# Second attention gathered and normalised sequence by sequence, first experts in 39 slots with the low weights in halves

## The chip, the core and the metric

The kernel runs on one core of a Trainium2 chip. The metric is the device time of one execution in microseconds (us). The engines are TensorE (PE, with its weight loads as PEld), VectorE (DVE), ScalarE (ACT), GpSimd (POOL) and SyncE (SP). SP only issues transfers here; POOL computes and also issues the indirect transfers. Each engine runs its own instructions in order, and engines meet through semaphores that count up.

## What is computed

Input x has 8 sequences of 512 tokens, 256 wide. Four blocks follow, each on a layer-normed x and each added to x:

```
x = x + attention0(norm(x))          softmax attention, 16 heads of 16
x = x + experts0(norm(x))            8 experts, 1024 wide, each token goes to its best 2
x = x + attention1(norm(x))          cosine attention with running sums, and a 1024-wide MLP
x = x + experts1(norm(x))            64 small experts (best 8), 2 shared ones

experts0: out[token] = share0 * y[expert0] + share1 * y[expert1]
          y[e] = gelu(x @ w1[e] + b1[e]) @ w2[e] + b2[e]

attention1 on z = norm(norm(x) by ln1):
  q, k = tanh(z W_Q) * pi/4, tanh(z W_K) * pi/4 ; V = z W_V
  heads = (cos q * cumsum(cos k * V) + sin q * cumsum(sin k * V)) / (cos q * cumsum(cos k) + sin q * cumsum(sin k) + 1e-6)
  mixed = norm(x) + heads W_O
  result = mixed + gelu(norm(mixed) W1 + b1) W2 + b2
```

All products are done at float32 accuracy from reduced-precision parts: each matrix is split in a high part (a rounded copy) and a low part (what is left), and three products hi*hi, hi*lo, lo*hi are summed.

## The kernel before, in words

Every block is a phase with its own buffers, and a phase begins when all engines have ended the one before. The whole x stays on chip as 32 tiles of 128 tokens. Two of the five phases matter here.

**First experts** (`experts0_phase`). The router has sorted the tokens by expert into a list in DRAM, `sorted_x`. Each expert's part of the list is filled up to whole slots of 256 rows; there are SLOTS = 40 slots, and slot n belongs to expert `slot_expert[n]`, read at run time. A loop of TURNS = 20 turns does two slots a turn (k = 0, 1). For one slot:

- SP (`load`) fetches for the next slot: w1 of 1 MB when its buffer has been split (`w1_split`), then the slot's rows (256 KB), b1, b2 (128 KB), and w2 of 1 MB when its buffer has been split (`w2_hi`, `w2_lo`). There is one raw buffer for w1 and one for w2.
- DVE splits w1 (L1067 high, L1074 low, 128x2048 in one instruction), splits the hidden values in four pieces (L1056 high, L1058 low), and adds b2 (L1080).
- ACT does the gelu (L1100) and the high half of w2 (L1108), which waits for w2 to land.
- POOL does the low half of w2 (L1028), which waits for ACT's high half, and then stores the slot's results to `sorted_y` (L1030).
- PE does the first product (L1128), turns the next slot's rows (L991), and does the second product (L1141).

The last turn also fetches and splits for a 41st slot that nobody computes.

**Second attention** (`attention1_phase`). It starts by collecting the experts' results: POOL issues 64 indirect gathers (L1326), two for each of 32 tiles, into the buffers `zn` and `mixed` used as a ring of four. DVE adds them to x, weighted by `share` (L1389, two a tile), and takes statistics (L1392), for all 32 tiles in turn; between the tiles it takes the low parts of the five weight matrices (L1383). Then come, for all tiles at once, the aggregation (L1398), the first guess of 1/sqrt(variance) (L69, L71), three Newton steps on POOL (L79 to L85, twelve instructions), and after them the pipeline. PE waits for all five weights before its first product.

The pipeline has 64 chunks (8 sequences, 8 chunks of 128 value channels each) and 78 stages; stage n works on chunk n. With s = n // 8 and c = n % 8, a stage holds on DVE six instructions of one chunk (L1492, L1498, L1508), on PE `value(n + 1)`, `up`, `down` and `weigh`, on ACT and POOL the splitting of `heads` and `hidden`. Beside them each sequence has a front (its norm on DVE L1428, turned by PE L1638, q and k, the denominator) and a back (mixed L1456, its statistics L1461, its norm L1475, the MLP), and their steps are put at fixed values of c: front of s + 2 normed at c = 7; front of s + 1 at c = 1, 3, 5; back of s - 1 at c = 1, 2, 3; the sum of s - 2 at c = 4.

What DVE may not overtake: `weigh_queries(n, 0)` writes over `weighted`, which POOL must have added up for chunk n - 2 (`heads_ready`, L1357).

## Time and profile before

| | us |
|---|---|
| three runs | 3191.21, 3200.32, 3200.80 |
| median | 3200.32 |
| the profiled execution's own time | 3190.54 |
| its span | 3188.8 |
| mean granted TensorE clock | 0.908 |

| busy | us | share |
|---|---|---|
| PE | 2539.1 | 80% |
| DVE | 1845.6 | 58% |
| ACT | 1238.0 | 39% |
| POOL | 983.2 | 31% |

| stretch of the span | what | length, us | PE busy, us |
|---|---|---|---|
| 0 to 714 | first attention | 714 | 572.39 |
| 714 to 887 | router and sorting | 173 | 44.91 |
| 887 to 1438 | first experts | 551 | 483.75 |
| 1438 to 1571 | second attention up to its first stage | 133 | 15.35 |
| 1571 to 2176 | second attention, pipeline and end | 605 | 455.39 |
| 2176 to 3188 | second experts | 1012 | 967.34 |

How to read it: times are from the span's start. A share of busy time is an average over stages with different limits, so the last table is the one to begin with. In a timeline row the numbers are start, duration, then engine, line, operation, output and inputs, and in brackets the idle time of that engine just before and what ended it. Busy PE is not PE at its peak, since its ends are modelled.

### The profile page before, as it was taken

What the parts mean: (1) busy time and instruction counts of PE and PEld (TensorE: products, weight loads), DVE (VectorE), ACT (ScalarE), POOL (GpSimd) and SP (SyncE); (2) the same over time, 40 slices, a digit from 0 to 9 for tenths busy, and PEclk for the clock granted to TensorE, in tenths of its full rate; (3) what the DMA queues carried; (4) which work ended last, traced back from release to release, by engine and by line L of the source; (5) the groups of instructions that cost most, each with busy time, mean ns of one, the idle gap of its engine ahead of it and who ended that gap; (6) DMA issues with size and microseconds to landing.
All of it is one profiled execution on the core that took longest, in us unless ns stands there. A gap on an engine that the chain in (4) does not pass through costs nothing. (4 is left out here: it accounts for less than half of the span.)

```text
span 3188.8 us, 51896 instructions
## 1 busy us (share of the span) xinstructions
PE 2539.1 (80%) x18615; PEld 2207.7 (69%) x18615; DVE 1845.6 (58%) x3241; ACT 1238.0 (39%) x1845; POOL 983.2 (31%) x1102
## 2 busy tenths in 40 slices
PE   1988888885069999980368777785999999999999
PEld 1777667765068888880256666675788888888888
DVE  5455555545057777775597777744744544544543
ACT  0444444442034444441123333332444444444444
POOL 3444445401734444437244444451000000000000
PEclk9899999985589999995589999997999999999999
DMA  2000000003256666654354554423422222221321
GB/s 80 1 2 2 1 1 1 1 11 128 97 179 209 211 213 212 211 193 145 94 139 126 130 129 123 123 57 116 146 97 79 86 84 77 89 81 66 100 78 60
DMA packets 195231, 317.13 MB, mean 99 GB/s; under 512 B 28757, under 2 KB 103449, under 8 KB 195097
## 3 DMA queue, kind: packets, MB, share of 16 engines
q1 hardware_dynamic: 182856, 277.00, 28.9%
q0 software_dynamic: 12240, 38.28, 3.5%
q8 instruction: 92, 1.51, 0.2%
q14 instruction: 43, 0.34, 0.0%
HBM read 274.83 MB, written 40.37 MB: 99 GB/s over the span
## 5 line engine op out<-in xcount | busy, mean ns | idle before, releaser
L2015 DVE TENSOR_TENSOR e_h_lo<-e_h,e_h_hi 128x512 fp32r<-128x512 f32 x320 | 221.6, 692 | 481.2 <-ACT e_h_hi L2081 481.0
L2068 ACT ACTIVATE e_h<-e_h_ps,e_b 128x512 f32<-128x512 f32 x320 | 220.3, 688 | 491.7 <-PE e_h_ps L2132 461.1
L2146 PE MATMUL e_y_ps<-e_w_hi,e_h_hi 128*128 128x256 f32 x1280 | 366.3, 286 | 22.8 <-DVE e_h_lo L2015 22.7
L2146 PE MATMUL e_y_ps<-e_w_hi,e_h_lo 128*128 128x256 f32 x1280 | 361.7, 283 | 0.0
L2146 PE MATMUL e_y_ps<-e_w_lo,e_h_hi 128*128 128x256 f32 x1280 | 361.5, 282 | 0.0
L1028 POOL TENSOR_TENSOR e_w_lo<-e_w,e_w_hi 128x2048 fp32r<-128x2048 f32 x40 | 186.5, 4662 | 315.1 <-ACT e_w_hi L1108 315.1
L2146 PEld LDWEIGHTS e_y_ps<-e_w_hi,e_h_hi 128*128 128x128 f32 x1280 | 243.1, 190 | 54.5 <-DVE e_h_lo L2015 39.6
L2132 PE MATMUL e_h_ps<-e_yT_hi,e_w_hi 128*128 128x512 f32 x640 | 257.9, 403 | 2.5 <-DVE e_yT_lo L2001 2.5
L401 DVE TENSOR_REDUCE a_top<-a_ring 128x2 f32<-128x1024 f32 (+3 forms) x256 | 202.7, 819 | 90.2 <-PE a_ring L602 89.3
L2132 PE MATMUL e_h_ps<-e_yT_lo,e_w_hi 128*128 128x512 f32 x640 | 253.6, 396 | 0.0
L2132 PE MATMUL e_h_ps<-e_yT_hi,e_w_lo 128*128 128x512 f32 x640 | 253.1, 396 | 0.0
L2146 PEld LDWEIGHTS e_y_ps<-e_w_lo,e_h_hi 128*128 128x128 f32 x1280 | 243.1, 190 | 11.4
L2146 PEld LDWEIGHTS e_y_ps<-e_w_hi,e_h_lo 128*128 128x128 f32 x1280 | 244.4, 191 | 0.0
L79 POOL TENSOR_TENSOR e_newton<-e_rstd 128x4 f32<-128x4 f32 x24 | 6.1, 252 | 770.7 <-DVE e_rstd L71 769.4
L463 ACT ACTIVATE a_probs<-a_ring 128x1024 f32<-128x1024 f32 (+1 forms) x192 | 167.9, 883 | 139.9 <-PE a_ring L616 138.3
L2081 ACT ACTIVATE e_h_hi<-e_h 128x512 fp32r<-128x512 f32 x320 | 199.5, 623 | 46.1 <-DVE e_h L2012 44.3
L1128 PE MATMUL e_h_ps<-e_xT_hi,e_w_hi 128*128 128x256 f32 x640 | 183.7, 287 | 35.9 <-DVE e_w_lo L1074 30.9
L2012 DVE TENSOR_TENSOR e_h<-e_h,e_spread 128x512 f32<-128x512 f32 x256 | 175.3, 685 | 17.7 <-ACT e_h L2068 13.7
L1056 DVE CAST e_h_hi<-e_h 128x512 fp32r<-128x512 f32 x160 | 113.3, 708 | 118.3 <-ACT e_h L1100 113.3
L1141 PE MATMUL e_y_ps<-e_w_hi,e_h_hi 128*128 128x256 f32 x640 | 180.7, 282 | 0.5 <-DVE e_h_lo L1058 0.5
L1128 PE MATMUL e_h_ps<-e_xT_hi,e_w_lo 128*128 128x256 f32 x640 | 179.6, 281 | 0.0
L1128 PE MATMUL e_h_ps<-e_xT_lo,e_w_hi 128*128 128x256 f32 x640 | 179.5, 280 | 0.0
(364 smaller groups left out, 7078.1 us busy)
## 6 DMA issues: line engine op xcount, KB each, us to landing
e_w<-in_w SPq DMA_DIRECT2D x82, 1024.0 KB, 5.4
e_spread<-share_store SPq DMA_DIRECT2D x512, 128.0 KB, 2.9
a_keys<-rows_store SPq DMA_DIRECT2D x128, 256.0 KB, 5.1
a_queries<-rows_store SPq DMA_DIRECT2D x86, 256.0 KB, 4.5
a_running_hidden<-rows_store SPq DMA_DIRECT2D x42, 256.0 KB, 4.5
e_xs<-sorted_x SPq DMA_DIRECT2D x41, 256.0 KB, 4.9
sorted_x<-zeros POOLq DMA_DIRECT2D x10, 1024.0 KB, 16.9
sorted_y<-e_ys POOLq DMA_DIRECT2D x40, 256.0 KB, 4.8
```

Source lines behind the costliest of these rows:

```text
L401: dve.reduce_max(top[r % 2][:, tb, :], banks(k)[:, :, at:at + (tb + 1) * P], AX.X).then_inc(top_taken.sem, top_taken.tick())
L463: act.activation(probs[r % 3][:, :, B_AT[i]:B_AT[i] + B_WIDTH[i]], banks(k)[:, :, 0:B_WIDTH[i]], ACT.Exp).then_inc(probs_ready.sem, probs_ ...
L1028: pool.tensor_tensor(lo[:, :, :], w2[:, :, :], hi[:, :, :], ALU.subtract).then_inc(w2_lo.sem, w2_lo.tick())
L1056: dve.tensor_copy(h_parts[0][:, cut, :], h[:, cut, :]).then_inc(h_hi.sem, h_hi.tick())
L1128: last = pe.matmul(h_ps[:, at:at + SLOT_TOKENS], l, r, start=(m == 0), stop=(m == len(ops) - 1))
L1141: last = pe.matmul(y_ps[n][:, 0:D], h_parts[a][:, f, n * P:(n + 1) * P], w2_parts[k][w][:, f, :], start=(f == 0 and m == 0), stop=(f == FC ...
L2012: dve.tensor_tensor(h[:, c % 2, :], h[:, c % 2, :], spread[c % SPREADS][:, :], ALU.mult).then_inc(scaled.sem, scaled.tick())
L2015: dve.tensor_tensor(h_parts[c % 2][1][:, :], h[:, c % 2, :], h_parts[c % 2][0][:, :], ALU.subtract).then_inc(h_lo.sem, h_lo.tick())
L2068: act.activation(h[:, c % 2, :], h_ps[c % 2][:, :], ACT.Silu, bias=b1[:, c:c + 1]).then_inc(h_ready.sem, h_ready.tick())
L2081: act.activation(h_parts[c % 2][0][:, :], h[:, c % 2, :], ACT.Copy).then_inc(h_hi.sem, h_hi.tick())
L2132: last = pe.matmul(h_ps[c % 2][:, :], l, r, start=(m == 0), stop=(m == len(ops) - 1))
L2146: last = pe.matmul(y_ps[n][:, 0:D], h_parts[c % 2][a][:, n * P:(n + 1) * P], w2[b][:, c, :], start=False, stop=(c == CH - 1 and m == 2))
```

## The change

In the first experts:

- SLOTS is 39, the most that 8192 rows in 8 parts can need at 256 rows a slot. The loop runs 19 turns, and the 39th slot follows it, with no fetch and no split for a next one.
- The slot's rows are fetched first and have a semaphore of their own; they wait for PE to have turned the rows of the slot before. The transposes wait for the rows alone, no longer for b1 and b2.
- The low part of w1 is taken in two halves. PE begins a slot's first product after the first half, and waits for the second half before the fifth of eight hidden blocks.

In the second attention:

- Gathers, sums and statistics go by sequence of four tiles. Sequences 0 to 2 are done before the pipeline, sequence s + 3 during it: gathers on POOL at c = 4 and 5, sums on DVE at c = 5 and 6, spread at c = 7; its Newton steps at the next c = 0, its centre at c = 2.
- Both norms go from DVE to ACT, as scale and bias (bias from a small DVE instruction, `centre`, `centre2`): the front's at c = 7, the back's at c = 2 behind the angles.
- The five raw weights have buffers of their own and are all fetched at once. Their splits are spread: wqk, wv, wo before the pipeline, w1 and w2 at stages 1 to 4. PE waits for each where it first uses it.

Between first attention and router POOL clears a range of semaphores, so that their numbers can be used again.

```diff
-SLOTS = TOKENS * 2 // SLOT_TOKENS + E0
+SLOTS = (TOKENS * 2 + E0 * (SLOT_TOKENS - 1)) // SLOT_TOKENS
...
         def load(sp, slot, kn, free):
+            free("x")
+            sp.dma_start(xs[kn][:, :, :], rows_in[...]).then_inc(x_loaded.sem, 16)
             free("w1")
             sp.dma_start(w1[:, :, :], t["w1_0"][...]).then_inc(w1_loaded.sem, 16)
             free("rest")
-            sp.dma_start(xs[kn][:, :, :], rows_in[...]).then_inc(rest_loaded[kn].sem, 16)
...
-                        if what == "w1":
-                            sp.wait_ge(w1_split.sem, w1_split.at(2 * k, i))
+                        if what == "x":
+                            sp.wait_ge(x_transposed.sem, x_transposed.at(k, i))
+                        elif what == "w1":
+                            sp.wait_ge(w1_split.sem, w1_split.at(3 * k, i))
...
-                    dve.tensor_tensor(lo[:, :, :], w1[:, :, :], hi[:, :, :], ALU.subtract).then_inc(w1_split.sem,
-                            w1_split.tick())
+                    for f in halves:
+                        low_half(f)
...
+                for b in range(BANKS):
+                    if b in (0, BANKS // 2):
+                        pe.wait_ge(w1_split.sem, w1_split.at(3 * k - (b == 0), i))
...
+            with pe.Fori(0, TURNS) as i:
+                for k in range(2):
+                    slot(k, i, True)
+            slot(0, TURNS, False)
...
+            def gather(s, tiles):
+                for n in tiles:
+                    if s >= 4:
+                        pool.wait_ge(trB.sem, trB.at(KC, s - 4))
+                        pool.wait_ge(x_plus.sem, x_plus.at(TB, s - 4))
+                    elif s:
+                        pool.wait_ge(combined.sem, combined.at(4 * (n // 2 + 1), s - 1))
+                    for k in range(2):
+                        row = s * TB + n
+                        pool.indirect_dma_start(out=got(n, k), ...).then_inc(gathered[n].sem, 16)
...
+            gather(0, range(TB))
+            gather(1, range(2))
+            refine_front(0)
+            gather(1, range(2, TB))
+            gather(2, range(2))
+            refine_front(1)
+            gather(2, range(2, TB))
+            refine_front(2)
...
+                if c == 0 and s >= 1 and live(s + 2):
+                    refine_front(s + 2)
+                if c == 4 and live(s + 3):
+                    gather(s + 3, range(2))
+                if c == 5 and live(s + 3):
+                    gather(s + 3, range(2, TB))
...
+                if n in (2, 4):
+                    low_weights(3 if n == 2 else 4)
+                if c == 5 and live(s + 3):
+                    combine(s + 3, LEFT)
+                if c == 6 and live(s + 3):
+                    combine(s + 3, RIGHT)
+                if c == 7 and live(s + 3):
+                    spread_of(s + 3)
+                if c == 2 and s >= 1 and live(s + 2):
+                    centre_of(s + 2)
...
+            def norm_front(s):
+                act.wait_ge(centred.sem, centred.at(1, s))
+                if s:
+                    act.wait_ge(trF.sem, trF.at(KC, s - 1))
+                for n in range(TB):
+                    act.activation(zf[:, n, :], g.x[:, s * TB + n, :], ACT.Identity, bias=token(centre, s, n),
+                                   scale=token(twice, s, n)).then_inc(znF.sem, znF.tick())
...
+                if c == 2 and live(s - 1):
+                    norm_back(s - 1)
+                if c == 7 and live(s + 2):
+                    norm_front(s + 2)
```

**SyncE, loop of the first experts, one slot.** Before, the weights w1 go first, then the rows `e0_xs1`, the biases and w2:

```order
L976 DMA e0_w1<-in_w1_0 128x2x1024
L979 ISA
L979 DMA e0_xs1<-sorted_x 128x2x256
L981 ISA
L981 DMA e0_b1_1<-in_b1_0 128x8
```

Now the rows stand ahead of w1:

```order
L981 DMA e0_xs1<-sorted_x 128x2x256
L1011 ISA
L984 ISA
L984 DMA e0_w1<-in_w1_0 128x2x1024
L1017 ISA
L987 ISA
L987 DMA e0_b1_1<-in_b1_0 128x8
```

The rows moved from behind w1 to ahead of it, so in the queue they now follow the w2 of the slot before.

**VectorE, from the last gathered tile to the first stage of the second attention.** Before (the 31 tiles ahead of this one read the same), the spread of all 32 tiles follows the last tile, and then the front of sequence 0:

```order
L1389 SCALAR_TENSOR_TENSOR x<-a1_zn,share0,x 128x256
L1389 SCALAR_TENSOR_TENSOR x<-a1_mixed,share1,x 128x256
L1392 BN_STATS a1_stats<-x 128x6
L1396 COPY a1_half<-a1_stats 128x1
L1398 BN_AGGR a1_mv<-a1_stats 128x2 x32
...
L1428 TENSOR_SCALAR a1_values_heads<-x,a1_mv,a1_inverse 128x256 x4
L1434 TENSOR_TENSOR a1_frontT0_lo<-a1_yT,a1_frontT0_hi 128x512 x2
L1439 SCALAR_TENSOR_TENSOR a1_run<-a1_ones,a1_trig 48x512
L1442 TENSOR_TENSOR a1_run<-a1_trig,a1_run 48x512
L1447 RECIPROCAL a1_den<-a1_den 48x512
L1449 TENSOR_TENSOR a1_den<-a1_trig,a1_den 48x512
```

Now, from the centre of sequence 0 on (`a1_frontT0_lo` belongs to its front, the sums around it to sequences 1 and 2):

```order
L1483 SCALAR_TENSOR_TENSOR a1_centre<-a1_mv,a1_inverse 128x4
...
L1464 BN_STATS a1_stats<-x 128x6 x2
L1469 COPY a1_half<-a1_stats 128x1
...
L1495 TENSOR_TENSOR a1_frontT0_lo<-a1_yT,a1_frontT0_hi 128x512 x2
L1450 TENSOR_TENSOR a1_wv_lo<-a1_weighted,a1_wv_hi 128x2048
...
L1460 SCALAR_TENSOR_TENSOR x<-a1_zn,share0,x 128x256 x2
L1460 SCALAR_TENSOR_TENSOR x<-a1_mixed,share1,x 128x256 x2
L1464 BN_STATS a1_stats<-x 128x6 x2
L1500 SCALAR_TENSOR_TENSOR a1_run<-a1_ones,a1_trig 48x512
```

The front of sequence 0 starts after 4 tiles instead of 32, and the sums and statistics of sequences 1 and 2 stand between its steps.

**GpSimd, two stages of the pipeline (c = 4 and 5).** Before, a stage is the hidden split, the sum of the heads and their split:

```order
L1349 TENSOR_TENSOR a1_hidden_parts<-a1_running_hidden,a1_hidden_parts 128x512
L1357 TENSOR_TENSOR a1_values_heads<-a1_weighted 128x512
L1360 TENSOR_TENSOR a1_head_parts<-a1_values_heads,a1_head_parts 128x512
L1349 TENSOR_TENSOR a1_hidden_parts<-a1_running_hidden,a1_hidden_parts 128x512
L1357 TENSOR_TENSOR a1_values_heads<-a1_weighted 128x512
```

Now four gathers follow in each of the two:

```order
L1403 TENSOR_TENSOR a1_hidden_parts<-a1_running_hidden,a1_hidden_parts 128x512
L1411 TENSOR_TENSOR a1_values_heads<-a1_weighted 128x512
L1414 TENSOR_TENSOR a1_head_parts<-a1_values_heads,a1_head_parts 128x512
L1368 DMA a1_zn<-sorted_y,row0 128x256
L1368 DMA a1_mixed<-sorted_y,row1 128x256
L1368 DMA a1_zn<-sorted_y,row0 128x256
L1368 DMA a1_mixed<-sorted_y,row1 128x256
L1403 TENSOR_TENSOR a1_hidden_parts<-a1_running_hidden,a1_hidden_parts 128x512
L1411 TENSOR_TENSOR a1_values_heads<-a1_weighted 128x512
```

The sum of the heads, for which DVE waits two stages later, now stands behind four gathers.

## Rows read from the trace of the kernel before

**Rows 1.** Busy time by stretch: length, then PE, PEld, DVE, ACT, POOL.
```profile
887.00:1438.00 551.00, 483.75 (x4004) 467.94 (x4004) 406.00 (x523) 259.03 (x422) 218.99 (x83) 0.98 0.63 205
1438.00:1571.00 133.00, 15.35 (x38) 7.82 (x38) 69.84 (x169) 16.52 (x16) 70.45 (x76) 0.51 0.34 103
```

**Rows 2.** Waits in the first experts: total, times, longest, in us.
```profile
POOL e_w_lo L1028 <- ACT e_w_hi L1108: 315.1, 40, 9.0
PE e_h_ps L1128 <- DVE e_w_lo L1074: 30.9, 37, 1.0
```

**Rows 3.** Timelines of the engines, one slot of the first experts.
```profile
1183.81 0.38 SPq L984 DMA_DIRECT2D e_w<-in_w  x1
1189.75 2.28 DVE L1074 TENSOR_TENSOR e_w_lo<-e_w,e_w_hi 128x2048 fp32r<-128x2048 f32 x1
1190.16 1.92 ACT L1108 ACTIVATE e_w_hi<-e_w 128x2048 fp32r<-128x2048 f32 x1 [3.64 <-DMA e_w<-in_w]
1192.16 4.61 POOL L1028 TENSOR_TENSOR e_w_lo<-e_w,e_w_hi 128x2048 fp32r<-128x2048 f32 x1 [7.81 <-ACT e_w_hi L1108]
1192.26 0.38 PE L1128 MATMUL e_h_ps<-e_xT_hi,e_w_hi 128*128 128x256 f32 x1 [0.91 <-DVE e_w_lo L1074]
```

**Rows 4.** Issue to landing: w1 (L976), rows (L979), w2 (L984), gathers (L1326).
```profile
DMA to landing us min/median/max: 4.8/4.9/5.7
DMA to landing us min/median/max: 3.7/4.9/5.5
DMA to landing us min/median/max: 5.0/6.2/8.5
DMA to landing us min/median/max: 2.7/2.8/7.1
```

**Rows 5.** Timelines, end of the experts and start of the second attention.
```profile
1427.92 0.75 DVE L1080 TENSOR_TENSOR e_ys<-e_y_ps,e_b 128x256 f32<-128x256 f32 x2
1432.64 0.72 POOL L1030 DMA_DIRECT2D sorted_y<-e_ys  x1
1439.94 1.01 POOL L1326 DMA_INDIRECT a_zn<-sorted_y,row  x1 [6.57 <-POOLq L933]
```

**Rows 6.** Timelines of VectorE and GpSimd, gathers and first front.
```profile
1450.32 0.48 DVE L1389 SCALAR_TENSOR_TENSOR x<-a_zn,share,x 128x256 f32<-128x256 f32 x1 [4.66 <-DMA a_mixed<-sorted_y,row]
1466.05 2.28 DVE L1383 TENSOR_TENSOR a_wv_lo<-a_values_heads,a_wv_hi 128x2048 fp32r<-128x2048 f32 x1
1466.60 2.54 POOL L1326 DMA_INDIRECT a_mixed<-sorted_y,row  x1 [0.30 <-issue]
1524.68 0.94 POOL L1326 DMA_INDIRECT a_mixed<-sorted_y,row  x1 [0.30 <-issue]
1537.56 1.38 DVE L1428 TENSOR_SCALAR a_values_heads<-x,a_mv,a_inverse 128x256 f32<-128x256 f32 x4
1553.86 1.22 DVE L1439 TENSOR_TENSOR_SCAN a_run<-a_ones,a_trig 48x512 f32<-48x512 f32 x1 [9.45 <-ACT a_trig L1575]
1558.61 3.35 DVE L1447 RECIPROCAL a_den<-a_den 48x512 f32<-48x512 f32 x1 [2.81 <-ACT a_den L1579]
1571.14 0.70 DVE L1492 TENSOR_TENSOR a_run_ps<-a_v_ps,a_keys 128x512 f32<-128x512 f32 x1 [7.17 <-DMA a_keys<-rows_store]
```

**Rows 7.** Timelines of VectorE and GpSimd, one sequence in the pipeline.
```profile
1771.41 1.64 DVE L1456 SCALAR_TENSOR_TENSOR a_mixed<-x,a_inverse,a_wo_ps 128x256 f32<-128x256 f32 x4
1772.98 1.39 DVE L1461 BATCH_NORM_STATS2 a_stats<-a_mixed 128x6 f32<-128x256 f32 x4
1788.64 0.69 DVE L1508 TENSOR_TENSOR a_weighted<-a_run_ps,a_queries 128x512 f32<-128x512 f32 x1 [4.17 <-POOL a_values_heads L1357]
1806.57 1.27 POOL L1360 TENSOR_TENSOR a_head_parts<-a_values_heads,a_head_parts 128x512 fp32r<-128x512 f32 x1 [0.74 <-ACT a_head_parts L1612]
1825.62 0.69 DVE L1508 TENSOR_TENSOR a_weighted<-a_run_ps,a_queries 128x512 f32<-128x512 f32 x1 [2.34 <-POOL a_values_heads L1357]
1827.35 1.36 DVE L1428 TENSOR_SCALAR a_values_heads<-x,a_mv,a_inverse 128x256 f32<-128x256 f32 x4
```

More of the change, by code:

```diff
@@ L1021, in _, with store_slot @@
                                ALU.subtract).then_inc(w2_lo.sem, 1)
-            with pool.Fori(0, TURNS) as i:
-                for k in range(2):
+            def store_slot(k, i, slot, more):
+                if more:
                     pool.wait_ge(w2_hi.sem, w2_hi.at(k + 1, i))
@@ L1108, in _ @@
                     act.activation(w2_parts[1 - k][0][:, :, :], w2[:, :, :], ACT.Copy).then_inc(w2_hi.sem, w2_hi.tick())
+            with act.Fori(0, TURNS) as i:
+                for k in range(2):
+                    slot(k, i, True)
                 for sem in (h_ready, w2_hi, x_hi):
                     sem.close()
+            slot(0, TURNS, False)
         @block.tensor
         def _(pe):
-            pe.wait_ge(rest_loaded[0].sem, rest_loaded[0].at(0))
+            pe.wait_ge(x_loaded.sem, x_loaded.at(0))
@@ new lines, in combine @@
+            def combine(s, tiles):
+                first = 2 * tiles[0]
+                for k in range(2):
+                    for i, n in enumerate(tiles):
+                        if k == 0:
+                            dve.wait_ge(gathered[n].sem, 32 * (s + 1))
+                        else:
+                            dve.wait_ge(combined.sem, combined.at(first + i + 1, s))
+                        dve.scalar_tensor_tensor(out=g.x[:, s * TB + n, :], in0=got(n, k), scalar=token(g.share[k], s, n),
+                                                 in1=g.x[:, s * TB + n, :], op0=ALU.mult, op1=ALU.add).then_inc(combined.sem)
+                for i, n in enumerate(tiles):
+                    dve.wait_ge(combined.sem, combined.at(first + len(tiles) + i + 1, s))
+                    dve.bn_stats(stats[:, s % 2 * TB + n, :], g.x[:, s * TB + n, :]).then_inc(stat_step.sem)
@@ L1674, in up @@
             def up(u):
+                if u == 0:
+                    pe.wait_ge(split.sem, split.at(4))
                 if u % FC1 == 0:
```

374 lines of the change are left out of this document (209 added, 165 removed).

## The prediction, written before the changed kernel was timed

> **What bounds the kernel now.** I read the busy time by stretch first, since the two edited phases have different limits. The first experts last 551 us and TensorE is busy for 484 of them; the second attention spends 133 us before its first stage, with TensorE busy for 15 [rows 1]. So the first is close to TensorE's own pace, and in the second TensorE all but stands still, for which the timelines must give the cause.
>
> In the experts the waits come next. TensorE waits 37 times, 30.9 us in all, for the low part of w1; GpSimd waits 40 times for ScalarE's high part of w2 [rows 2]. The timelines of one slot tell which of the two sets the pace. w2 is asked for at 1183.81 and ScalarE can begin on it at 1190.16, 6.35 later; GpSimd's low part starts 2.00 after that and takes 4.61, and only when it ends may the next w2 be asked for [rows 3]. 6.35 + 2.00 + 4.61 and some 0.1 for the last step are 13.1 us, and 40 times that is 524 of the phase's 551 us. This ring of one raw w2 buffer goes round at its own pace; TensorE, which waits 0.91 in the slot shown [rows 3], is not in it.
>
> In the second attention I follow the chain back from the first stage at 1571.14. It waits 7.17 for the spread keys, and before that come the reciprocal at 1558.61, the running sum at 1553.86 (9.45 idle ahead of it) and the norm at 1537.56 [rows 6]. From norm to first stage are 33.6 us. Ahead of the norm stand the 64 gathers, from 1439.94 [rows 5] to 1524.68 [rows 6], 84.7 us, one every 1.25 when undisturbed (0.94 and 0.30 idle). GpSimd's gathers bound this stretch, and nothing of them is needed beyond the first four tiles to begin sequence 0.
>
> In the pipeline the timeline of VectorE shows where its work is covered: it waits 4.17 for the sum of the heads at 1788.64 (c = 3) and 2.34 at 1825.62 (c = 7) [rows 7].
>
> **The change, part by part.** The sum is made against the profiled execution's own 3190.54. The three runs lie at 3191 to 3201, so the profile is at their lower end, and a median of new runs may come up to 10 above my number.
>
> *One slot less.* The ring's 13.1 us go once: -13.1.
>
> *End of the experts.* Before, the last results were ready at 1428.67 (1427.92 + 0.75), but the store was issued at 1432.64, behind the low part of a w2 that nobody used [rows 5]. Now it follows at once: -4.0. The unrolled last slot is new code on every engine; no row shows its fetch. Bounds 0 and 4 (the longest fetch could be no longer than the 6.57 idle at the phase's start [rows 5], less what the barrier takes); I take +1.
>
> *w1 in halves.* TensorE can start a slot up to 1.0 earlier. What is late next is the ring above: GpSimd's low part of w2 cannot move, and VectorE and the second product follow it. So the gain is had once, not in every slot: -1.1. Both ends for the range: nothing, and 30.9 us if the ring shortens too (a rival). The w1 fetch waits for the second half, which ends when the whole did.
>
> *Rows ahead of w1.* They are now asked for behind the previous w2, in the same queue. Before, w1 and the rows issued right behind it both landed 4.9 after their issues, with w1 four times as large [rows 4]: the queue works them off in order, the rows last. Behind w2 they would then cost w2 nothing, and I take 0. The Trainium skill, "DMA: Bandwidth & Descriptors" (section "Queues, rings and completion order"), says that each transfer engine takes the descriptors of one ring in order; by this rule too the sum gets nothing here, and the rival below in which rows and w2 share would be out. I keep that rival, since no row shows this order of issue.
>
> Experts: -13.1 - 4.0 + 1 - 1.1 = -17.2.
>
> *Second attention up to the first stage.* The eighth gather is issued 7 x 1.25 after 1439.94, at 1448.7. Tile 1, whose last gather went out at 1443.7, was summed only at 1450.32 [rows 6], 6.6 later instead of the usual 2.8 [rows 4], because the weights were in flight; now five weights instead of three are asked for at once, so I add 3.8 for the eighth as well. From the last gather (1524.68) to the norm (1537.56) passed 12.9 us [rows 6]; with 28 fewer aggregations I estimate 10.9. The norm starts at 1448.7 + 3.8 + 10.9 = 1463.4. On ScalarE four tiles cost between 1.0 (half of the 1.92 for 128x2048, [rows 3]) and 2.0; I take 1.9 against VectorE's 1.38: +0.5. So the front moves by 1463.4 + 0.5 - 1537.56 = -73.7.
>
> Its cover: sums of sequences 1 and 2 now stand between its steps on VectorE. Sequence 1's second pair is gathered only behind GpSimd's Newton steps: four gathers from 1463.4, the last landing 3.75 + 2.8 later at 1470; two sums and statistics (about 2, [rows 7]) and a spread (1.2, estimate) bring 1473, where the low parts of the front would have begun near 1469.5. That is +3.5. Sequence 2's stand ahead of the reciprocal and cost about 0.5; the rest falls in the 9.45 and 7.17 of waiting. Gain before the first stage: -73.7 + 4.0 = about -70. Bounds: -60 (each of the two later groups late by one Newton and four gathers) and -76.
>
> *In the pipeline,* five sequences get eight sums (2 x 1.64), four statistics (1.4), a spread (1.2) and small centres (0.5): 6.4 us of VectorE each [rows 7]. The front's norm of 1.36 goes from c = 7 [rows 7]. The back's goes too, but it and the centres lie ahead of the 4.17 wait, so they count nothing. The 2.34 wait at c = 7 disappears under the new work. 6.4 - 0.5 - 1.4 - 2.3 = 2.2; I add 0.5 for the wait on the last gather's landing and 0.8 since ScalarE must do the back's norm behind the angles, late for the next hidden chunk: +3.5, four times. In sequence 0 no hidden chunks run, there is nothing to absorb, and two low weights of 2.28 each [rows 6] come in: 6.0 - 1.4 + 4.6 = +9. On GpSimd the four gathers (5.0) start when the heads' split ends at 1807.84 (1806.57 + 1.27, [rows 7]) and end at 1812.8, when the next hidden split is due about then. Total +23; bounds +5 (all else absorbed) and +73 (both groups of gathers exposed, below).
>
> Second attention: -70 + 23 = -47. Clearing semaphores and one transfer less of zeros are not on a path that the router waits for: 0.
>
> Sum: 3190.5 - 17.2 - 47 = 3126.
>
> **Rivals.**
>
> *The ring shortens too.* If w2 lands sooner because the rows no longer run ahead of it (its landings span 5.0 to 8.5, [rows 4]), the slot falls from 13.1 toward TensorE's own 12.1. Against it: w2 takes 6.2 at the median, also where w1 went out earlier. At 12.3 and 38 slots: -30, 3096. Chance 0.13.
>
> *Rows and w2 share.* The rows, a quarter of w2's size, delay it by up to a quarter of 4.9; at half of that, 0.6 in 38 slots: +23, 3149. Against it the in-order landing above. Chance 0.09.
>
> *GpSimd binds at c = 4 and 5.* If the sum of the heads behind the gathers is late, VectorE waits 5 us twice in each of five sequences: +50, 3176. For it: the 2.34 and 4.17 waits show that these sums are late already. Against it: VectorE itself gets 4.8 us more there. Chance 0.11.
>
> *The other side: gathers held up by VectorE.* A gather took 2.54 instead of 0.95 when it was issued inside a VectorE instruction of 2.28 [rows 6]. In the pipeline VectorE is nearly always in an instruction. If each of 8 gathers takes 2.84 with its gap, that is 22.7 us a sequence on GpSimd, of which I let 4 be covered: +93, 3219, slower than before. It decides from about 1.9 us of exposed time per gather. Against it: the instructions there are under 1.3 us long but for the reciprocal. The Trainium skill, "SBUF — State Buffer" (section "Who interferes with whom"), says that copies, casts and tensor-scalar forms can lock GpSimd out, and that a tensor-tensor does not stop descriptor writing. By that rule the gathers at c = 4 and 5 would run free and this rival would be out; the row disagrees, since what ran there was a tensor-tensor [rows 6], and the measurement decides. Chance 0.05.
>
> **How the numbers follow.** Forecast 0.62, the rivals 0.13, 0.09, 0.11 and 0.05. The time is the forecast's, 3126. Its own range is 3112 to 3142. The whole range, 3085 to 3168, takes in the first two rivals and leaves out the last two, 0.16. A measurement of this kernel can tell about 0.3%, 9.6 us, from no change. All cases but the last are faster: 0.94; same 0.02; slower 0.04.
>
> **What would show it.** Right: 39 low parts of w2 some 13.1 apart; TensorE's wait on w1's low part gone and found again ahead of the second product; the store right behind the last sums; first stage about 62 us after the first gather; sequences 1 to 4 of the pipeline 3 to 4 us longer than before, sequence 0 about 9. Wrong: slots clearly under 12.8 or over 13.4; gathers in the pipeline above 1.5 us; VectorE waits on the heads of over 4 us at c = 6 or 7; or a first stage later than 75 us after the first gather.

## The result, and the profile after

| | kernel before | changed kernel |
|---|---|---|
| runs, median | 3191.2 us (9 runs, 3182.6 to 3200.8) | 3168.1 us (9 runs, 3159.4 to 3183.3) |
| ratio, 95% interval | | 0.9928 (0.9905 to 0.9952) |
| profiled execution, its span | 3190.5, 3188.8 us | 3170.1, 3168.3 us |

The change is worth about 23 us by the medians, 15 to 30 by the interval; the forecast was 3126 us, a gain of 64, and its range ended at 3168. So the prediction was wrong in size: two thirds of the gain did not come.

To find where it went I cut each trace at the same three instructions: SP's first fetch of the first experts, GpSimd's first gather, and VectorE's first instruction of the last phase.

| us | before | after | difference | forecast |
|---|---|---|---|---|
| up to the first experts (not edited) | 887.4 | 884.2 | -3.2 | 0 |
| first experts, to the first gather | 552.6 | 540.4 | -12.2 | -17.2 |
| first gather to first stage | 131.2 | 61.2 | -70.0 | -70 |
| first stage to the last phase | 605.0 | 669.5 | +64.5 | +23 |
| last phase (not edited) | 1012.7 | 1013.0 | +0.3 | 0 |

The first row is no part of the change: over the fourteen profiles of this study this unedited stretch took 876 to 897 us. That is much of why whole times of one kernel spread by 20 us and more, and why I compare the stretches. The edited ones give 17.7 of the 20.5 us between the two profiles.

A stretch repeats better, but not exactly. The unedited attention took 736.2 before and 741.1 in e3_experts_only below; of kernels that share one attention, the changed kernel, e4 and e8 took 730.7, 731.2 and 728.4. So a difference of a few us between two profiles needs a second sign, such as a wait that went or a chunk that shrank.

The busy time by stretch of the changed kernel (length, then PE, PEld, DVE, ACT, POOL, granted clock, DMA share, GB/s), for the experts and the stretch up to the first stage, answers to [rows 1]. TensorE is busy for 480 of the 540 us of the experts, as it was for 484 of 551, and still for only 14 us ahead of the first stage, but of 61 instead of 133:

```profile
884.10:1424.50 540.40, 479.75 (x3900) 462.03 (x3900) 442.17 (x551) 246.50 (x409) 206.90 (x80) 0.97 0.60 200
1424.50:1485.80 61.30, 13.96 (x38) 7.02 (x38) 32.97 (x91) 16.52 (x22) 34.00 (x60) 0.56 0.44 137
```

The waits in the experts (total, times, longest) answer to [rows 2]. TensorE's wait for w1's low part is gone from the list, and one of the same size stands ahead of the second product instead. In e8_no_halves below it is the other way round (32.8 for the first product, 2.9 for the second), so the halves only moved it.

```profile
POOL e_w_lo L1034 <- ACT e_w_hi L1130: 302.9, 38, 10.6
PE e_y_ps L1170 <- DVE e_h_lo L1070: 34.8, 72, 0.9
```

The timelines of the start of the second attention (start, length, engine, line, operation, idle time before and what ended it) answer to [rows 5, 6]. The store goes out at 1417.45, behind the last sum; the first norm, now ScalarE's, begins 23.4 us after the first gather (forecast 23.5) and takes 2.07; the first stage follows 61.2 us after the gather (forecast 62).

```profile
1417.45 0.71 POOL L1036 DMA_DIRECT2D sorted_y<-e_ys  x1 [7.30 <-DVE e_ys L1096]
1424.59 1.01 POOL L1368 DMA_INDIRECT a_zn<-sorted_y,row  x1 [6.43 <-POOLq L935]
1447.95 2.07 ACT L1648 ACTIVATE a_values_heads<-x,a_centre,a_inverse 128x256 f32<-128x256 f32 x4 [18.02 <-DVE a_centre L1483]
1473.58 3.35 DVE L1507 RECIPROCAL a_den<-a_den 48x512 f32<-48x512 f32 x1
1485.83 0.70 DVE L1551 TENSOR_TENSOR a_run_ps<-a_v_ps,a_keys 128x512 f32<-128x512 f32 x1 [5.84 <-DMA a_keys<-rows_store]
```

The loss is in the pipeline. I took the start of VectorE's first instruction of each chunk (L1492 before, L1551 after) and wrote down the distance to the next one. Sequence 3, in us; each kernel's name stands for its experiment below:

```
                   c=0   c=1   c=2   c=3   c=4   c=5   c=6   c=7   sequence
before             4.6  15.3   5.9  16.0   9.4   8.8   4.6   9.4     74.0
after              4.6  15.5   4.8  19.1   9.6  17.8   6.9   7.0     85.3
e1_sums_later      4.6  17.9   4.8  17.7   9.5   8.9   6.9  11.5     81.8
e2_back_norm       4.6  15.5   6.1  16.8  10.0  18.3   6.9   7.0     85.2
e5_stats_in_wait   4.6  17.3   4.8  19.0   9.8   8.8   6.2  10.4     81.0
e6_stats_and_norm  4.6  15.7   6.1  16.7  10.1   8.8   6.2  10.2     78.5
e7_no_sums         4.6  17.0   4.8  17.6   9.5   8.9   5.7  12.2     80.4
e9_gathers_earl.   4.6  15.5   4.8  19.0   9.5  11.3   6.9   6.8     78.5
e10_all_earlier    4.6  15.7   6.1  16.8   9.8   8.9   6.2   7.5     75.6
```

Sequences 2 and 4 of the changed kernel differ from this by at most 0.9 in a chunk. Chunk 5 alone is 9.0 longer than before, 8.9 in sequence 2. The timeline of VectorE and GpSimd there, in sequence 2, shows it at work:

```profile
1675.65 0.97 POOL L1368 DMA_INDIRECT a_zn<-sorted_y,row  x1
1676.93 0.95 POOL L1368 DMA_INDIRECT a_mixed<-sorted_y,row  x1 [0.30 <-issue]
1678.09 1.22 DVE L1557 TENSOR_TENSOR_SCAN a_v_ps<-a_ones,a_v_ps 128x512 f32<-128x512 f32 x1
1684.01 1.25 DVE L1460 SCALAR_TENSOR_TENSOR x<-a_zn,share,x 128x256 f32<-128x256 f32 x1 [4.70 <-DMA a_mixed<-sorted_y,row]
1686.47 0.48 DVE L1460 SCALAR_TENSOR_TENSOR x<-a_zn,share,x 128x256 f32<-128x256 f32 x1 [1.21 <-DMA a_mixed<-sorted_y,row]
1686.87 0.88 DVE L1460 SCALAR_TENSOR_TENSOR x<-a_mixed,share,x 128x256 f32<-128x256 f32 x2
1687.66 0.74 DVE L1464 BATCH_NORM_STATS2 a_stats<-x 128x6 f32<-128x256 f32 x2
1688.32 3.32 DVE L1507 RECIPROCAL a_den<-a_den 48x512 f32<-48x512 f32 x1
1692.29 0.68 DVE L1551 TENSOR_TENSOR a_run_ps<-a_v_ps,a_keys 128x512 f32<-128x512 f32 x1
```

The gather itself takes 0.95, as in the stretch ahead of the pipeline. But the rows of tile 0, asked for at 1676.93, are there only at 1684.0, and the first sum stands in VectorE's row ahead of the reciprocal and of chunk 6. Two waits, 4.70 and 1.21, and the sums and statistics of two tiles, 1.64 + 0.74, are 8.3 of the 8.9. TensorE stands still with it; from its timeline, and the busy time by stretch from 1675 on:

```profile
1693.62 0.80 PE L1737 MATMUL a_v_ps<-a_frontT_hi,a_wv_hi 128*128 128x512 f32 x1 [11.29 <-DVE a_weighted L1567]
```
```profile
1675.00:1684.00 9.00, 6.41 (x38) 5.58 (x38) 4.31 (x6) 1.95 (x3) 7.12 (x8) 1.00 0.74 161
1684.00:1691.50 7.50, 0.00 (x0) 0.00 (x0) 6.29 (x7) 0.00 (x0) 4.79 (x5) 0.59 0.31 89
1691.50:1700.00 8.50, 6.38 (x21) 5.23 (x22) 8.46 (x16) 0.82 (x2) 0.00 (x0) 0.56 0.38 114
```

TensorE does nothing in the 7.5 us, and the granted clock, at its upper level (2.4 GHz, 1.00) before, is 0.59 and 0.56 in this stretch and the next, near its lower level (1.2 GHz): the first product takes 0.80, where the one at 1675.92 took 0.51.

Why the rows come late has two parts. One is in the transfers issued from 1675.0 to 1680.5, and from 1685.0 to 1690.0 (KB each, median us from issue to landing):

```profile
a_running_hidden<-rows_store SPq DMA_DIRECT2D x2, 256.0 KB, 5.8
a_keys<-rows_store SPq DMA_DIRECT2D x2, 256.0 KB, 7.0
a_zn<-sorted_y,row POOLq DMA_INDIRECT x2, 5.6
a_mixed<-sorted_y,row POOLq DMA_INDIRECT x2, 7.0
```
```profile
a_zn<-sorted_y,row POOLq DMA_INDIRECT x2, 2.8
a_mixed<-sorted_y,row POOLq DMA_INDIRECT x2, 2.8
```

Beside four spreads of queries and keys, 1 MB together, a gather lands in 5.6 to 7.0 us. The second group, with no spread beside it, lands in 2.8, the number of [rows 4] that I had worked with. SP sends spreads out once a chunk, behind VectorE; the second group went out while VectorE stood still. At 1761 to 1765, in sequence 3, the first group reads 6.0 and 6.8. That the spreads slow the rows is read from such coincidences; no run takes the spreads away.

The other part is that the gathers are issued too late for the sums, whatever the landing. Sequence 1 shows it by itself. Its first group went out 6.0 us after the start of chunk 5 (1.1 in sequences 2 to 4), with no spread issued beside it, and VectorE waited 4.30 all the same (the gathers of 1592 to 1598, then the rows of GpSimd and VectorE):

```profile
a_zn<-sorted_y,row POOLq DMA_INDIRECT x2, 3.2
a_mixed<-sorted_y,row POOLq DMA_INDIRECT x2, 2.8
```
```profile
1594.25 0.95 POOL L1368 DMA_INDIRECT a_mixed<-sorted_y,row  x1 [0.30 <-issue]
1597.04 3.86 DVE L1460 SCALAR_TENSOR_TENSOR x<-a_zn,share,x 128x256 f32<-128x256 f32 x2 [4.30 <-DMA a_mixed<-sorted_y,row]
1597.73 1.27 POOL L1403 TENSOR_TENSOR a_hidden_parts<-a_running_hidden,a_hidden_parts 128x512 fp32r<-128x512 f32 x1
```

In sequence 2 VectorE stood ready at 1679.31, and the second gathers of the two tiles went out at 1676.93 and 1679.44. With 2.8 to each landing it would have waited 0.4 and then 2.1, so 2.5 of the 5.9 (an estimate from these rows). Done for all five sequences this gives 14.7 of the 28.0 us that VectorE waits for rows in the pipeline: about half is the slow landing and about half the late issue.

### The profile page after: what moved, and what is told of

The parts are those of the page before. It is cut to its first block and busy times, and to the rows that moved or that the text cites. A ratio compares the mean times of both kernels' runs of the same rounds, so it can differ in the third digit from the quotient of the medians.

```text
span 3168.3 us, 51829 instructions
## 1 busy us (share of the span) xinstructions
PE 2551.7 (81%) x18511; PEld 2213.6 (70%) x18511; DVE 1859.1 (59%) x3264; ACT 1256.2 (40%) x1896; POOL 987.4 (31%) x1182
## 5 line engine op out<-in xcount | busy, mean ns | idle before, releaser
L1034 POOL TENSOR_TENSOR e_w_lo<-e_w,e_w_hi 128x2048 fp32r<-128x2048 f32 x38 | 175.6, 4622 | 302.9 <-ACT e_w_hi L1130 302.9
L2270 PEld LDWEIGHTS e_y_ps<-e_w_lo,e_h_hi 128*128 128x128 f32 x1280 | 243.4, 190 | 11.3
L1068 DVE CAST e_h_hi<-e_h 128x512 fp32r<-128x512 f32 x156 | 153.3, 983 | 71.7 <-ACT e_h L1122 67.1
L2136 DVE TENSOR_TENSOR e_h<-e_h,e_spread 128x512 f32<-128x512 f32 x256 | 175.3, 685 | 17.8 <-ACT e_h L2192 13.6
L1737 PE MATMUL a_v_ps<-a_frontT_hi,a_wv_hi 128*128 128x512 f32 x128 | 62.6, 489 | 141.1 <-DVE a_weighted L1567 141.0
```

The lines of the kernel that those rows point to most:

```text
L1034: pool.tensor_tensor(lo[:, :, :], w2[:, :, :], hi[:, :, :], ALU.subtract).then_inc(w2_lo.sem, w2_lo.tick())
L1068: dve.tensor_copy(h_parts[0][:, cut, :], h[:, cut, :]).then_inc(h_hi.sem, h_hi.tick())
L2136: dve.tensor_tensor(h[:, c % 2, :], h[:, c % 2, :], spread[c % SPREADS][:, :], ALU.mult).then_inc(scaled.sem, scaled.tick())
L2270: last = pe.matmul(y_ps[n][:, 0:D], h_parts[c % 2][a][:, n * P:(n + 1) * P], w2[b][:, c, :], start=False, stop=(c == CH - 1 and m == 2))
```

## The experiments

The kernel before ran beside them: 20 runs at 3186.3 us (median) beside the first four kernels, 9 at 3190.8 beside the next four, 7 at 3189.5 beside the last four. Ratios are to these, each with its 95% interval. In the paragraphs below "attention" is the stretch from the first gather to the last phase (736.2 before, 730.7 after), "experts" the one ahead of it (552.6 and 540.4).

**e1_sums_later.**

```
-                if c == 5 and live(s + 3):      combine(s + 3, LEFT)
-                if c == 6 and live(s + 3):      combine(s + 3, RIGHT)
-                if c == 7 and live(s + 3):      spread_of(s + 3)
+                if c == 6 and live(s + 3):      combine(s + 3, LEFT)
+                if c == 7 and live(s + 3):      combine(s + 3, RIGHT); spread_of(s + 3)
```

> The changed kernel with the sums of a sequence's rows on VectorE one chunk later: first two tiles after chunk 6, last two and the spread after chunk 7; gathers stay after chunks 4 and 5 on GpSimd. Theory A (VectorE stands at the gathers' landing, 4.2 + 1.2 us in each of five sequences, with everything behind it): the interval that begins at chunk 5 falls from 17.7 to about 11, five sequences gain 5 to 7 us each, and the kernel comes to about 3168 - 30 = 3138 us. Theory B (GpSimd binds: its four gathers, 5.0 us, hold up the sum of the heads and the split of the hidden chunk): the wait only moves from the gathers' landing to the heads' sum, VectorE waits 4 to 6 us for the heads in chunk 5 or 6, and the kernel stays at 3160 to 3170 us.

Measured 3149.6 us, 0.9878 (0.9842 to 0.9915); attention 717.3, 13.4 less than after. The landing wait fell from 28.0 to 5.3 us in the pipeline, and chunk 5 returned to 8.9. So the wait was real and did not simply move to the heads, against B. But A's 30 did not come either: chunk 7 grew by 4.5 and the next chunk 1 by 2.4. Moving the sums only moved them to where they are not hidden.

**e2_back_norm_vector.** The four ScalarE norms of the back (`norm_back`) are four tensor-scalar operations on VectorE again, as in the kernel before.

> The changed kernel with the second norm of each sequence back on VectorE (four tensor-scalar operations instead of ScalarE's four, and no centre). Theory A (ScalarE's norm stands ahead of the hidden chunk and the high parts in its row, and costs 1.5 to 3 us in each sequence at chunks 2 and 3): about 8 to 12 us faster than the changed kernel, 3157 us, and VectorE's wait for the high part of the back channels falls from 23.8 to about 9 us. Theory B (the longer stage at chunk 3 comes from elsewhere, ScalarE's time is covered): within 3 us of the changed kernel.

Measured 3166.2 us, 0.9931 (0.9899 to 0.9963), no different from the changed kernel as a time. By the trace the attention is 6.3 shorter (724.4): chunk 3 shorter by 2.3 to 3.2, chunk 2 longer by 1.2 (2.5 in sequence 1), and the wait for the high part of the back channels 11.6 instead of 23.8. The mechanism is A's by the chunks and the wait; its size, a little under the 8 to 12 expected, is known to a few us only, and the wait for rows grew meanwhile from 28.0 to 32.9.

**e3_experts_only.** `attention1_phase` of the kernel before, all else as changed.

> The kernel before with the edits of the first experts alone (39 slots, rows asked for first, low weights in halves); the second attention is the old one. If the two parts of the change add up, this is 12 us faster than the kernel before (the ring at 13.2 us goes round once less, -13.2; store earlier -3.7; a slower start and a slightly slower ring +5), 3179 us, and the attention's part is the remaining -11. My forecast had -17 for this part. A rival: the clock or the memory of the attention depends on what ran ahead, and this part alone is worth over 17 or under 8.

Measured 3178.6 us, 0.9974 (0.9956 to 0.9992). The experts took 543.0, 9.6 less than before. The time is 7.7 us less than that of the kernel before beside it, where 12 were expected and under 8 was the rival's; the unedited attention took 4.9 more than in the profile before, and I can't tell this from the spread of that stretch. So the parts add up roughly, and the experts are not worth 17.

**e4_rows_behind_w1.** In `load`, the rows' transfer stands behind w1's again.

> The changed kernel with the rows asked for behind w1 as before; halves and 39 slots stay. Theory A (rows asked for between w2 and w1 take part of the transfer time of w2 and of the first w1): the ring goes round in 13.12 instead of 13.19 us and the first slots start 1.5 to 2 us earlier, 3 to 5 us in all, and w2's wait on ScalarE falls back from 4.9 to about 3.6 us per slot. Theory B (transfers of one queue come strictly one after the other): the ring's period stays at 13.19, and nothing changes by over 1 us, or it gets slower since the transposes wait for the rows again.

Measured 3173.6 us, 0.9967 (0.9946 to 0.9988). In the trace the experts took 540.4, exactly as in the changed kernel: ring 13.16 instead of 13.18, ScalarE's wait for w2 142 instead of 181 us, the second step 21.1 instead of 19.5. So the order of rows and w1 is worth nothing. The wait fell as A has it, but not for A's reason: w2 landed 6.2 us after its issue at the median, 6.3 in the changed kernel, and ScalarE waits just 145 us in e8, where the rows are ahead too. The long wait comes only with halves and rows ahead together, and the ring does not follow it. Against its own comparison this kernel gains 12.7 us where the changed kernel gained 23.1. The 10 us between them are not in any stretch that was edited; the unedited first one took 2.9 us more in this profile than in that of the changed kernel, and where the rest came from I leave open.

**e5_stats_in_wait.** As e1, but `combine` of sequences 3 to 7 only sums, and

```
                 if c == 1 and live(s + 1):
                     front(s + 1, m, "low0")
+                    if s >= 1 and live(s + 2):
+                        stats_of(s + 2, range(TB)); spread_of(s + 2)
                     front(s + 1, m, "low1")
  (GpSimd)
-                if c == 0 and s >= 1 and live(s + 2):   refine_front(s + 2)
+                if c == 1 and s >= 1 and live(s + 2):   refine_front(s + 2)
```

> The kernel of the first experiment (sums after chunks 6 and 7), and in addition the statistics and the spread of the sequence that is three ahead stand after chunk 1 of the next sequence, between the two low parts of the front channels, where VectorE waits 3.5 us for ScalarE; GpSimd's Newton steps for them follow at chunk 1 instead of chunk 0. Theory A (with the landing wait gone, VectorE is the bound of chunks 5, 6, 7 and 0, every instruction there costs its length, while chunks 1 and 3 have waits to hide it in): chunk 7's interval falls from 11.5 to about 8.5 and chunk 1's from 17.9 to 15.5, 5 us in each of four to five sequences, 3128 us. Theory B (GpSimd's row binds: hidden split, heads, Newton steps in order): the heads of chunk 1 come later by the 3.4 us of the steps, and the kernel stays within 5 us of 3149.

Measured 3142.1 us, 0.9834 (0.9786 to 0.9882); attention 706.0, 11.3 less than e1. The wait for the front's high part fell from 19.6 to 4.8 us: the statistics are hidden there. Half of what A expected came; chunk 7 stayed at 10.4.

**e6_stats_and_norm.** e5 with e2's norm.

> The kernel of the fifth experiment with the second norm back on VectorE, as in the second experiment. There it shortened the pipeline by about 1.2 us in each sequence (chunk 3 shorter by 2.4, chunk 2 longer by 1.2). If that adds up, this is 6 to 9 us faster than the fifth experiment, 3120 us; a rival: VectorE has no wait left at chunk 2 and 3 once the statistics moved, and it is no faster.

Measured 3136.3 us, 0.9829 (0.978 to 0.9877); attention 701.2. It adds up in part, 4.8 by the stretch, which is no more than the unedited attention moved in e3; the chunks go the way they went in e2: in sequences 2 to 4 chunk 3 is shorter by 0.8 to 2.3 and chunk 2 longer by 1.2.

**e7_no_sums.** In e1's `combine`, for s >= 3: a copy of one element in place of the sum.

> The kernel of the first experiment without the eight sums (scalar-tensor-tensor, 128x256) of each of sequences 3 to 7: a copy of one element stands for each, so gathers, waits, statistics and all else stay, and the results of these sequences are those of the rows without the experts' share. It prices the sums. Theory A (VectorE binds there): 8 x 0.41 less 8 x 0.06 = 2.8 us a sequence, five times, 14 us, about 3135 us. Theory B (GpSimd's gathers bind): within 3 us of the first experiment, 3147 to 3150.

Measured 3148.0 us, 0.9854 (0.9806 to 0.9901); attention 710.5, 6.8 less than e1. 14 us of VectorE's work were taken away and half of it came back. Chunk 7 of sequence 3 did not shrink, 12.2 (in sequences 2 and 4 it lost 0.9), VectorE's wait for the heads grew from 48.0 to 52.6 us, and its wait for the rows, which the small copies keep, from 5.3 to 10.2. So VectorE met GpSimd's results and the landing earlier, and waited for both: neither theory alone.

**e8_no_halves.** The changed kernel with `halves = [slice(0, F0)]` and the semaphore's counts to match.

> The changed kernel with the low part of w1 in one instruction of 128x2048 again; 39 slots and rows first stay. Theory A (the ring of w2 sets the pace, halves are worth one step at most, and the slow start of the experts comes from how VectorE's and GpSimd's low parts meet): ring still 13.1 to 13.2 us, TensorE waits 0.8 us a slot for w1's low part again, and the time is within 3 us of the changed kernel. Theory B (the halves do shorten something in every slot): 5 to 10 us slower.

Measured 3160.8 us, 0.9912 (0.987 to 0.9953). Experts 536.3: 4.1 *less* than with the halves, where I expected none. The timelines of VectorE and GpSimd in the second slot, first the changed kernel, then e8:

```profile
910.81 4.55 POOL L1034 TENSOR_TENSOR e_w_lo<-e_w,e_w_hi 128x2048 fp32r<-128x2048 f32 x1 [7.94 <-ACT e_w_hi L1130]
911.10 6.47 DVE L1074 TENSOR_TENSOR e_w_lo<-e_w,e_w_hi 128x1024 fp32r<-128x1024 f32 x2
917.50 0.74 DVE L1096 TENSOR_TENSOR e_ys<-e_y_ps,e_b 128x256 f32<-128x256 f32 x2
917.75 0.37 SPq L984 DMA_DIRECT2D e_w<-in_w  x1
```
```profile
907.96 2.29 DVE L1074 TENSOR_TENSOR e_w_lo<-e_w,e_w_hi 128x2048 fp32r<-128x2048 f32 x1
907.99 6.73 POOL L1034 TENSOR_TENSOR e_w_lo<-e_w,e_w_hi 128x2048 fp32r<-128x2048 f32 x1 [8.26 <-ACT e_w_hi L1130]
910.42 0.37 SPq L984 DMA_DIRECT2D e_w<-in_w  x1
```

The two halves should take 2.35 and took 6.47: one of them lasted 5.34 and ended with GpSimd's low part. In e8 VectorE was 0.03 ahead and GpSimd waited. w1's fetch, which waits for the split, goes out 6.65 after VectorE's start in the one and 2.46 in the other. In the nine other kernels with halves the pair took 6.36 to 6.78 too, also where VectorE's first half came first: then GpSimd got in between the halves and the second waited. The next low part of w2 came after 19.2 to 19.6 us (21.1 in e4) with halves, and after 15.2 to 15.5 without (16.3 in the kernel before). In later slots the two are not due together, and it costs nothing.

**e9_gathers_earlier.** One difference to the changed kernel:

```
-                if c == 4 and live(s + 3):   gather(s + 3, range(2))
-                if c == 5 and live(s + 3):   gather(s + 3, range(2, TB))
+                if c == 3 and live(s + 3):   gather(s + 3, range(2))
+                if c == 4 and live(s + 3):   gather(s + 3, range(2, TB))
```

> The changed kernel with one difference: GpSimd issues the gathers of the pipeline after chunks 3 and 4 instead of 4 and 5; VectorE's sums stay after chunks 5 and 6. Theory A (the loss at chunk 5 is the landing of rows gathered too late): VectorE's wait of 5.4 us a sequence for the gathers goes, chunk 5's interval falls from 17.7 to 11.5, and the kernel gains some 25 to 30 us of the pipeline, less what sums at chunk 5 cost, 3140 us. Theory B (GpSimd binds): its row is as long as before, the heads of chunk 4 come late instead, chunk 4 grows by 3 to 5 us, and the gain is under 12 us.

Measured 3135.2 us, 0.9838 (0.9812 to 0.9865); attention 702.8, 27.9 less than the changed kernel. It is A's number, and the largest effect of one edit here. VectorE's waits in the pipeline from 1485 to 2000 us (total, times, longest), of the changed kernel and of e9:

```profile
DVE a_weighted L1567 <- POOL a_values_heads L1411: 41.7, 16, 6.0
DVE x L1460 <- DMA a_mixed<-sorted_y,row: 28.0, 9, 4.7
```
```profile
DVE a_weighted L1567 <- POOL a_values_heads L1411: 45.4, 18, 5.9
DVE x L1460 <- DMA a_mixed<-sorted_y,row: 2.9, 2, 1.8
```

The heads wait 3.7 us more over the whole pipeline, and chunk 4 did not grow. The wait for rows fell by 25.1. This profile has no landing times, but by the two waits that are left, in sequences 0 and 1, rows still took 6.3 and 7.0 us (asked for at 1514.3 and 1579.1). So the landing can be as slow as it was; the earlier issue hides it. In e9's chunk 5 the same instructions run without a gap:

```profile
1663.29 1.22 DVE L1557 TENSOR_TENSOR_SCAN a_v_ps<-a_ones,a_v_ps 128x512 f32<-128x512 f32 x1
1664.41 0.85 DVE L1460 SCALAR_TENSOR_TENSOR x<-a_zn,share,x 128x256 f32<-128x256 f32 x2
1665.19 0.87 DVE L1460 SCALAR_TENSOR_TENSOR x<-a_mixed,share,x 128x256 f32<-128x256 f32 x2
1665.98 0.74 DVE L1464 BATCH_NORM_STATS2 a_stats<-x 128x6 f32<-128x256 f32 x2
1666.64 3.33 DVE L1507 RECIPROCAL a_den<-a_den 48x512 f32<-48x512 f32 x1
```

**e10_all_earlier.** e6 with e9's gathers.

> The kernel of the sixth experiment (sums after chunks 6 and 7, statistics at chunk 1, back norm on VectorE) with GpSimd's gathers after chunks 3 and 4 instead of 4 and 5. Without the sums at all chunk 7 still took 10.6 to 12.2 us, so something of GpSimd is in it: its five us of gathers after chunk 5 push the heads of chunks 6 and 7. Theory A (that is so): chunk 7 falls from 10.2 to about 8, chunk 6 stays at 6.2, and 2 us are gained in each of five sequences, about 10 us, 3126 us. Theory B (chunk 7 is bound by VectorE and TensorE alone): no gain, 3133 to 3138 us.

Measured 3128.0 us, 0.9815 (0.9785 to 0.9846); attention 688.4, 12.8 less than e6. Chunk 7 fell from 10.2 to 7.5, A's number, but the timeline does not show A's mechanism. VectorE and GpSimd in chunk 7 of sequence 3, first e6, then e10:

```profile
1759.49 0.69 DVE L1572 TENSOR_TENSOR a_weighted<-a_run_ps,a_queries 128x512 f32<-128x512 f32 x1 [0.70 <-POOL a_values_heads L1411]
1763.58 0.69 DVE L1460 SCALAR_TENSOR_TENSOR x<-a_zn,share,x 128x256 f32<-128x256 f32 x1 [1.89 <-DMA a_mixed<-sorted_y,row]
1763.93 1.46 POOL L1411 TENSOR_TENSOR a_values_heads<-a_weighted 128x512 f32<-128x512 f32 x1
1764.19 1.88 DVE L1460 SCALAR_TENSOR_TENSOR x<-a_mixed,share,x 128x256 f32<-128x256 f32 x2
```
```profile
1754.76 0.69 DVE L1572 TENSOR_TENSOR a_weighted<-a_run_ps,a_queries 128x512 f32<-128x512 f32 x1 [0.90 <-POOL a_values_heads L1411]
1757.27 0.87 DVE L1460 SCALAR_TENSOR_TENSOR x<-a_mixed,share,x 128x256 f32<-128x256 f32 x2
```

The heads are waited for as long as before, 0.70 and 0.90. What went is the wait for rows, 1.89, and the stretching of the sums: the last two take 1.88 beside a GpSimd tensor-tensor in e6 and 0.87 in e10. On average over sequences 2 to 4, chunk 7 loses 1.6 of waiting for rows and 1.5 of longer sums. Later sums fall together with GpSimd's work, and earlier rows take them out of its way. That they meet is read from the timelines; no run parts the two.

**e11_no_halves.** e6 with e8's edit.

> The kernel of the sixth experiment with w1's low part in one instruction. The halves cost 4 us once, in the second slot of the experts (GpSimd's low part of w2 got in between them, and VectorE's second half took 5.3 us instead of 1.2): without them the third low part of w2 follows the second after 15.5 instead of 19.5 us, and the kernel is 4 us faster than the sixth experiment, 3131 us. A rival: the 4 us come back as a wait later in the ring, and the time is the same.

Measured 3130.7 us, 0.9815 (0.9797 to 0.9834). Experts 535.0, 5.1 less than in e6, so the gain of e8 is there again and does not come back as a wait; the attention is 702.6, as in e6.

**e12_both.** e10 with e8's edit.

> The tenth and eleventh experiments together: sums after chunks 6 and 7, statistics at chunk 1, back norm on VectorE, gathers after chunks 3 and 4, w1's low part in one instruction. If both add to the sixth experiment: 3121 us, some 70 us less than the kernel before. A rival: gathers after chunk 3 wait for the transposes of the back norm and hold up the heads of chunk 4, and it is no better than the eleventh.

Measured 3117.7 us, 0.9773 (0.9752 to 0.9794), 72 us less than the kernel before: the best version found. Experts 534.6, attention 689.5, so both parts are there. The rival is out: this kernel is 13 us faster than e11, and chunk 4 takes 9.5 to 9.7 in sequences 2 to 4, where it takes 9.9 to 10.1 in e11. The ratio to the changed kernel is 0.9773 / 0.9928 = 0.984, by way of the kernel before, since the two did not run side by side.

## Why the prediction was wrong

*One slot less, store, new code: right in sum.* -13.1 by the ring, which went round in 13.18 us against 13.12. The store followed the last sum (1416.39 + 0.76) after 0.3, where it had been 4.0 late. Two small misses cancel, which was luck: 0.06 more a turn is 2.2 us over the slots, and from the last low part of w2 that was used to the first gather passed 5.2 us less than before, where I had 4.0 less and 1 more for new code. No cost of new code shows there.

*w1 in halves: wrong sign.* I took -1.1, once. It cost 4.1, once, in the second slot. Nothing in [rows 3] shows it, since there VectorE's low part had ended when GpSimd's began; I priced a split as harmless without asking who uses the pause. The trace of the kernel before had the warning in its second slot: GpSimd's low part, begun 0.11 us behind VectorE's, took 6.66 instead of 4.62. The experts without halves came to -16.3 (e8), against -16.1 in my sum, so this is the whole of what they missed.

*Rows ahead of w1: right, 0.* e4's stretch is the same to 0.1, and w2 landed as soon with the rows ahead of it.

*Up to the first stage: right.* -70 forecast, -70.0 measured, and with the steps in between: norm 23.4 after the first gather.

*In the pipeline: this step failed.* +23 forecast, +64.5 measured. It failed in two sentences. The first was "I add 0.5 for the wait on the last gather's landing". VectorE waits 4.3 to 6.7 us a sequence for rows, 28.0 in all, and e9, which changes nothing but the issue of the gathers, takes 27.9 away. I had looked only at when GpSimd would have issued the gathers and at the last one. The first pairs decide, because the first sums stand in VectorE's row ahead of the reciprocal and of the next chunk. Even at the 2.8 of [rows 4] they would have come some 2.5 us late in a sequence; and they travel with 1 MB of spreads and take up to 7.1, which is the other half. I had even used a row with this behaviour, the landing of 6.6 "because the weights were in flight", for the start and not for the pipeline.

The second was that ScalarE's norm of the back costs 0.8, in four sequences. With it on ScalarE a sequence is longer by about 1.2 at chunks 2 and 3, in the later sequences too (e2: 6.3 in all).

What is left, 64.5 - 27.9 - 6.3 = 30.3, stands against the rest of my sum: 23 less four times 0.5 + 0.8 is 17.8. These 12.5 us are not settled. Some of them are in sequences 5 to 7 and the end, which take in no rows and for which I had put nothing: they are 7.1 longer than before, and e2 takes about 3 of these away. Some may be VectorE's sums, which I priced at 0.41 each: the first of sequence 1, in the rows above, lasted 3.47 beside GpSimd's tensor-tensors (the pair of sums is the 3.86 of the row). Some may be no more than the spread of the stretch.

By sequence the sum was not bad once the gathers are in time. In e9 sequences 0 to 4 are 11.2, 5.9, 5.1, 4.5 and 4.2 longer than before, where I had 9 and four times 3.5; in the changed kernel it is 12.9 (8.4 of it at chunk 5), 11.3, 11.7, 11.3 and 10.2.

*The rivals.* "GpSimd binds at c = 4 and 5" gave 3176, near the time, and I had 0.11 on it. That it came near is luck, since its mechanism is not the one that decided: VectorE's wait for the heads in the pipeline grew by 6.6 us, from 47.5 to 54.1, not by 50, and the wait for rows is new. In one way GpSimd is in it, since it issued the gathers late (sequence 1). "Gathers held up by VectorE" is out: they took 0.94 to 1.20. "Ring shortens" and "rows and w2 share" are out: the ring is as it was, and so is the landing of w2. I had no rival in which VectorE waits for the rows. Under "what would show it" I named waits on the heads and long gathers, but not a wait of VectorE on the transfer.

The forecast for the attention, -47, was reached by e10 (-47.8). That it agrees to the microsecond is chance, since e10 also hides the statistics (e5), which my sum had not. But the gain was to be had; it was the placement that gave it back.

## What to carry to other kernels

When a transfer is moved from a quiet stretch into a pipeline, look at which instruction waits for its first bytes, when that instruction is ready, and what is queued behind it, and price the landing with what else is in flight there. A move of the issue by one step cost nothing and was worth 28 us; moving the consumer instead was worth half (13.4), since it landed in a part where its engine had no slack and GpSimd was at work. Find the slack first (chunks of 15 to 19 us had it, those of 4.6 had none) and put there what may go anywhere. Cutting an instruction in two opens a door between the parts, and another engine may come in by it.

## What the runs showed of the hardware

A low part on VectorE and one on GpSimd (tensor-tensor, both inputs on chip) do not run at the same time. The one that begins second lasts until the first has ended, and then its own time: 6.73 instead of 4.62 on GpSimd in e8, 5.34 instead of 1.22 on VectorE after the change, with 0.03 to 0.4 us between the starts. The Trainium skill, "SBUF — State Buffer" (section "Who interferes with whom"), says that a VectorE instruction with two such inputs contends with a GpSimd instruction that reads, and that the order of issue decides who blocks; these rows agree. The sums (scalar-tensor-tensor, 128x256) are stretched by GpSimd's tensor-tensors too: the first of sequence 1 in the changed kernel lasted 3.47 instead of 0.48, from 1597.04 to 0.3 after the second of two tensor-tensors (1597.73 and 1598.95) had ended. A gather issued just behind a VectorE tensor-tensor of 128x2048 is held too; e9, in sequence 0:

```profile
1509.66 2.26 DVE L1450 TENSOR_TENSOR a_w_lo<-a_arrived_w,a_w_hi 128x2048 fp32r<-128x2048 f32 x1
1509.71 3.04 POOL L1368 DMA_INDIRECT a_mixed<-sorted_y,row  x1 [0.31 <-issue]
```

It took 3.04 instead of 0.95, like the 2.54 of [rows 6]. In the changed kernel no gather took over 1.20; beside two sums of 128x256 some took 1.64 in e6. The same section says, as inferred, that a tensor-tensor does not keep GpSimd from writing descriptors; with rows like this one the measurement decides against it. I did not look for the operand that makes the difference.
